# Tiles of 127 edges that carry the running sum in a row of their own, in a graph layer with two aggregations

## The reference

```python
def _L0_gnn_ref(x, edge_index, edge_attr, Wn, bn, We, be, attn):
    src, dst = (edge_index[0], edge_index[1])
    h = x @ Wn.T + bn
    e = edge_attr @ We.T + be
    ...
    a = jax.nn.leaky_relu(jnp.sum((xj + ee) * attn, axis=-1), NEG_SLOPE)
    m = jax.ops.segment_max(a, dst, num_segments=N)
    a = jnp.exp(a - m[dst])
    denom = jax.ops.segment_sum(a, dst, num_segments=N)
    a = a / (denom[dst] + 1e-16)
    msg = (xj * a[..., None]).reshape(-1, H * C)
    out = jax.ops.segment_sum(msg, dst, num_segments=N)
    return jax.nn.relu(out)

def _L1_gnn_ref(x, W1, b1, W2, b2, edge_index):
    dst = edge_index[0]
    nbr = edge_index[1]
    agg = jax.ops.segment_sum(x[nbr], dst, num_segments=n)
    cnt = jax.ops.segment_sum(jnp.ones((nbr.shape[0],), x.dtype), dst, num_segments=n)
    mean = agg / jnp.maximum(cnt, 1.0)[:, None]
    return x @ W1.T + b1 + mean @ W2.T + b2
edge_index = jnp.stack([src, dst])
x = _layernorm(x + _L0_gnn_ref(x, edge_index, edge_attr_128, ...), axis=-1)
x = _layernorm(x + _L1_gnn_ref(x, ..., edge_index), axis=-1)
```

## Time and profile before

| what | value |
|---|---|
| time, median of 3 runs | 1420.48 us (1420.19 to 1420.97) |
| the profiled execution: own time, span | 1415.41 us, 1413.6 us |
| TensorE busy (matmuls), its granted clock | 1191.4 us (84%), 0.945 |
| DVE, ScalarE, Pool busy | 1066.7, 737.7, 751.0 us |
| stage over destinations | about 394 to 618 us |
| dense stage | about 618 to 1034 us |
| stage over sources | about 1034 to 1386 us |

### The profile page before, as it was taken

How to read it: one execution, slowest core, us unless ns; L and a number is a source line. 1 busy time by engine, 2 the same in 40 slices (tenths; PEclk the granted TensorE clock), 3 DMA queues, 4 the chain that set the end, 5 groups by cost and what they waited for, 6 DMA issues and landing times.

```text
span 1413.6 us, 25643 instructions
## 1 busy us (share of the span) xinstructions
PE 1191.4 (84%) x6726; PEld 1029.3 (73%) x6726; DVE 1066.7 (75%) x3862; ACT 737.7 (52%) x1768; POOL 751.0 (53%) x731
## 2 busy tenths in 40 slices
PE   4499867980079999949999999999989998889894
PEld 3388756870068888838888888888878887778783
DVE  8988876887465555439999999999988877676761
ACT  4756684540034444427777777777764444343441
POOL 1057761777767777754444203556541656555663
PEclk9899998995589999979999999999999999999997
DMA  5988798979436666556777768999971332322221
GB/s 187 274 220 211 181 284 240 302 239 378 157 57 95 95 91 102 71 123 234 243 238 244 250 241 276 320 323 331 321 250 55 100 94 77 93 84 93 88 77 44
DMA packets 118435, 260.94 MB, mean 185 GB/s; under 512 B 23531, under 2 KB 57148, under 8 KB 118360
## 3 DMA queue, kind: packets, MB, share of 16 engines
q1 hardware_dynamic: 75738, 193.82, 43.1%
q0 software_dynamic: 40128, 64.45, 19.9%
q10 hardware_dynamic: 2494, 1.84, 0.4%
HBM read 182.48 MB, written 130.49 MB: 221 GB/s over the span
## 4 chain that ended last, share of the span: by engine, by line
PE 54%; DMA 11%; POOL 10%; issue 9%; DVE 7%; ACT 7%; ACTq 0%; POOLq 0%; DVEq 0%
PE bank L1261 31%; PE bank L1250 8%; DMA xin<-z_scratch,idx_src 5%; PE bank L1238 5%; POOL out_rows L469 4%; POOL xin L466 4%; PE bank L1313 4%; PE bank L1309 4%; ACT aggn L607 3%; DVE X L752 2%; DMA X<-in_x,idx_src 2%; PE bank L1189 2%; DVE stats L935 2%; DMA yout<-low_digits_scratch 2%; ACT sel L655 1%
## 5 line engine op out<-in xcount | busy, mean ns | idle before, releaser
L1261 PE MATMUL bank<-w1T,xT 128*128 128x256 f32 x1968 | 459.2, 380 | 0.3 <-ACT yout L569 0.3
L1261 PEld LDWEIGHTS bank<-w1T,xT 128*128 128x128 f32 x1968 | 366.1, 190 | 47.5 <-issue 0.9
L475 POOL DMA_INDIRECT order_scratch<-pay,rank_i x200 | 194.6, 973 | 221.7 <-DVE xin L752 89.9
L935 DVE BATCH_NORM_STATS2 stats<-xin 128x6 f32<-128x512 f32 x246 | 158.7, 687 | 88.6 <-DMA xin<-z_scratch,idx_src 67.0
L559 ACT ACTIVATE xT<-bank 128x512 f32<-128x512 f32 x346 | 207.3, 600 | 19.8 <-PE bank L1250 11.5
L569 ACT ACTIVATE yout<-bank,rstd 128x256 f32<-128x256 f32 x492 | 204.9, 484 | 5.7 <-DVE rstd L1151 5.2
L668 ACT COPY agg<-bank 128x257 f32<-128x257 f32 (+1 forms) x200 | 74.3, 371 | 220.5 <-PE bank L1313 214.4
L935 DVE BATCH_NORM_STATS2 stats<-bank 128x6 f32<-128x512 f32 x246 | 168.2, 693 | 23.7 <-PE bank L1261 23.7
L514 POOL DMA_INDIRECT z_scratch<-xin,idx_out x100 | 156.5, 1565 | 53.4 <-ACT xin L681 30.2
L564 ACT ACTIVATE std<-stats,eps_c 128x4 f32<-128x4 f32 x271 | 80.6, 298 | 179.3 <-DVE stats L935 177.0
L469 POOL DMA_INDIRECT out_rows<-yout,idx_out x100 | 99.8, 998 | 138.2 <-DMA xin<-z_scratch,idx_src 72.7
(11 more groups left out here) (199 smaller groups left out, 1766.5 us busy)
## 6 DMA issues: line engine op xcount, KB each, us to landing
z_scratch<-in_x SPq DMA_DIRECT2D x125, 400.0 KB
xin<-z_scratch SPq DMA_DIRECT2D x97, 512.0 KB
out_rows<-yout SPq DMA_DIRECT2D x97, 512.0 KB, 3.3
yout<-keys_scratch SPq DMA_DIRECT2D x50, 256.0 KB, 5.2
kB<-sorted_scratch SPq DMA_DIRECT2D x50, 256.0 KB, 3.4
yout<-low_digits_scratch SPq DMA_DIRECT2D x50, 128.0 KB
xin<-in_edge_attr SPq DMA_DIRECT2D x12, 512.0 KB, 5.3
order_scratch<-pay,rank_i POOLq DMA_INDIRECT x200
```

What stands on the lines that cost most here:

```text
L475: g.indirect_dma_start(out=order_dram[k], out_offset=bass.IndirectOffsetOnAxis(ap=rank_i[k][:, t:t + 1], axis=0), in_=pay[:, t, :], in_off ...
L935: return v.bn_stats(stats[0:rows, slot, 2 * p:2 * p + 2, :].rearrange("p j s -> p (j s)"), pair.rearrange("p j c -> p c j"))
L1261: ins = mm(to, buf[:, jj, c, 0:n], w[:, c, :], start=not biased and i == 0 and c == 0, stop=i == len(terms) - 1 and c == 1)
```

## The change

- **Tiles of 127 edges.** The ranks are raised by one (`offs` plus one), so record 0 of the sorted order is empty, and `load_order` reads windows of 128 records that start every `TW` = 127: row 0 of a tile repeats the last edge of the tile before. There are 100 tiles still. Row 0 of `X` is overwritten with the running sum, with weight one: ScalarE's `carry_row` copies row 0 of the bank (1 partition by 257) into row 0 of the next tile of `X`. For that the key row that goes to DRAM for the columns (`krowo`) has the tile's last key in column 0, so the column 0 of the product is the running sum of the last key.
- **One product per tile.** `csel`, `agg`, `prevk`, `lastrow` and the second product are gone; `select` makes four matrices per group instead of eight.
- **Scaling from PSUM.** In the first aggregation DVE's `dst_mean` takes a tile at a time from the bank (addition, reciprocal, scaling). In the second, DVE makes the reciprocal only (`src_count`) and ScalarE scales (`mean`). The next use of the bank waits for this (`s_an`) instead of for a copy. The column of means is gone (`XW` = 257).
- **Order.** TensorE's aggregations are spread between turns and half products, ScalarE's and DVE's instructions are put in another order, with the outputs in two halves.
- **Pool waits a group behind.** In the source stage the gathers of group `q` wait for the landing of those of `q - 1`, and the scatters of `h` for the landing of those of `h - 1`; the wait for the gathers just issued is gone.

```diff
-XW = D + 2
+XW = D + 1
+TW = P - 1
...
+                o = order_dram[k]
+                windows = bass.AP(o.tensor, o.offset, [[TW * 3, T], [3, P], [1, 3]])
+                pool.dma_start(ordrow[:], windows).then_inc(s_ord, 16)
+
+            pool.wait_ge(s_zero, 112)
             load_order(DST)
...
+                    if q >= 1:
+                        pool.wait_ge(s_xs[(q - 1) % 4], 16 * GT * ((q - 1) // 4 + 1))
                     for j in range(GT):
                         gather(xin[(G + q) % 4][:, j, :], z_dram, column(idx_src[SRC], GT * q + j), s_xs[q % 4])
...
                     pool.wait_ge(s_ey, GT * h + GT)
-                    if q < Q:
-                        pool.wait_ge(s_xs[q % 4], 16 * GT * (q // 4 + 1))
+                    if h >= 1:
+                        pool.wait_ge(s_ysc[(h - 1) % 4], 16 * GT * ((h - 1) // 4 + 1))
...
-            def raw(k, q, u, j):
-                act.wait_ge(s_agg[k], q * GT + j + 1)
-                wait(act, s_an[k], 2 * (q - 1))
-                w = D + 1 + k
-                a.copy(agg[u % 2][:, j, 0:w], bank[2 + j % 2][:, 0:w]).then_inc(s_raw[k], 1)
+            def carry_row(k, q, j):
+
+                t = q * GT + j
+                if isinstance(t, int) and t == T - 1:
+                    return
+                act.wait_ge(s_agg[k], t + 1)
+                if k == SRC and j == GT - 1:
+                    act.wait_ge(s_sel[SRC], q + 2)
+                a.copy(X[0:1, bass.ds(t + 1, 1), :].rearrange("p a c -> p (a c)"),
+                       bank[2 + j % 2][0:1, 0:XW]).then_inc(s_raw[k], 1)
...
+                def mean(j):
+                    if in_range(q, 0, Q):
+                        if j % 2 == 0:
+                            wait(act, s_tb[SRC], 2 * (q - 1) + j // 2 + 1)
+                        act.wait_ge(s_den[SRC], q * GT + j + 1)
+                        a.activation(aggn[:, j, :], bank[2 + j % 2][:, 0:D], ACT.Copy,
+                                     scale=den[:, 1, j:j + 1]).then_inc(s_an[SRC], 1)
...
+                row(0)
+                cp(0)
+                row(1)
+                cp(1)
                 if in_range(q, 2, Q + 2):
...
+                    root(2 + u % 2, s_est, q - 1, s_esq)
+                mean(0)
+                mean(1)
+                row(2)
+                if in_range(q, 0, Q):
+                    root(u % 2, s_ost, q + 1, s_osq)
+                y_pair(0)
+                mean(2)
+                row(3)
+                mean(3)
+                y_pair(1)
+                if in_range(q, 0, Q - 2):
+                    root_neighbours(q + 2, u)
...
+            def dst_mean(q, j):
+
+                o = bank[2 + j % 2]
+                t = q * GT + j
+                free_bank(DST, t)
+                ts(den[:, 0, j:j + 1], o[:, D:XW], TINY, None, ALU.add).then_inc(s_den[DST], 1)
+                dve.wait_ge(s_den[DST], 2 * t + 1)
+                v.reciprocal(den[:, 1, j:j + 1], den[:, 0, j:j + 1]).then_inc(s_den[DST], 1)
+                if j % 2 == 0:
+                    wait(dve, s_tb[DST], 2 * (q - 1) + j // 2 + 1)
+                dve.wait_ge(s_den[DST], 2 * t + 2)
+                ts(aggn[:, j, :], o[:, 0:D], den[:, 1, j:j + 1], None, ALU.mult).then_inc(s_an[DST], 1)
+
+            def src_count(q, j):
+
+                free_bank(SRC, q * GT + j)
+                wait(dve, s_an[SRC], GT * (q - 1) + j + 1)
+                v.reciprocal(den[:, 1, j:j + 1], bank[2 + j % 2][:, D:XW]).then_inc(s_den[SRC], 1)
...
+                wait(pe, s_an[k], t - 1)
+                wait(pe, s_raw[k], t)
+                rows = X[:, bass.ds(t, 1), :].rearrange("p a c -> p (a c)")
+                mm(bank[2 + j % 2][:, 0:XW], sel[u % 2][:, j, :], rows, start=True, stop=True).then_inc(s_agg[k], 1)
...
+                agg_(0)
+                turn_b(0)
+                turn_x(0)
+                agg_(1)
+                turn_b(1)
+                turn_x(1)
+                prod(0, 0)
+                agg_(2)
+                prod(0, 1)
+                agg_(3)
+                prod(1, 0)
+                prod(1, 1)
             steps(pe, Q + 2, 4, 4, 3, by_src)
```

232 lines of the change are left out of this document (109 added, 123 removed).

## The result

The changed kernel takes 1335.53 us (median of 4 runs, 1332.91 to 1337.76), the kernel before 1420.34 us beside it (1418.86 to 1420.97): a ratio of 0.9404, 95% interval 0.9385 to 0.9422. The forecast was 1343 us in a range of 1329 to 1375. The execution that was profiled took 1335.28 us for a span of 1333.5 us.

What follows compares the result with a forecast made beforehand. TensorE paces destinations, close ahead of Pool; in the source stage no engine is full and gather landings stall Pool and DVE. 1415.4 - 19 - 57.7 - 1.5 + 0.5 = 1337.7, plus 5.1 to the median: 1343 us, range 1329 to 1375.

Steps and rivals of the forecast that it cites:

- preparation: Before the first aggregation: more small DVE steps when the sorted rows arrive, +0.5 us, bounds 0 and +2.
- destinations: Stage over destinations: Pool's 100 adds in a row, 1.87 us apart, set the pace; -19 us, bounds -15 to -21.
- source run-in: Source groups 0 and 1: wait for ScalarE in both versions, fewer selections and products give perhaps 1.5 us: -1.5.
- source groups: Source stage: 10.8 us a group instead of 13.31, over 23 groups, -57.7 us; bounds 10.4 and 12.1 a group.
- run-out: End of the source stage (turn, products, statistics, outputs, last scatters): no edit shortens it, 0 us.
- the step on the start: Start of the destination stage: cold first tiles wait for ScalarE either way; first add at about 410.5 instead of 412.23 us.
- this mechanism as a rival: Destination stage: TensorE's standing lowers its clock to 1.2 GHz throughout, +138 us, 1481 us in all; chance 0.04.
- The walk through the group: One source group, engine by engine: TensorE's last product ends at 10.7 us; ScalarE and DVE keep about 1 us.
- both waits are met on arrival: Pool, source stage: gathers land in 2.7 to 4.2 us, with 5.2 us of other issues between, so its moved waits cost nothing.
- In-order stalls in the source stage: Rival, source stage: DVE's first statistics 1.3 us late make a group 12.1 us, 1373 us in all; chance 0.18.
- Pool's instructions lengthen: Rival, source stage: all eight Pool instructions at the longest need 11.7 us a group, 1364 us in all; chance 0.07.
- The landing stays on the path: Rival, source stage: gathers reach DVE late, loop stays near 13.3 us, only destinations gain, 1400 us; chance 0.07.

Runs made afterwards that it cites:

- experiment 4: Changed kernel with two of Pool's four scatter-adds per destination group left out, so half the rows are not added: 1313.05 us, ratio 0.9241.
- experiments 8 and 9: Changed kernel plus unread bf16 products of zeros before and between TensorE's first aggregations, run twice: 1331.28 and 1331.22 us, against 1335.22 us for the changed kernel.
- experiment 3: Changed kernel with TensorE making every aggregation product twice into the same bank: 1399.42 us, ratio 0.9845.
- experiment 6: Changed kernel with ScalarE copying the running sum's row twice, first to a spare row: 1353.38 us, ratio 0.9517.
- experiment 1: Changed kernel with Pool's old wait back: source-stage scatters again wait for the gathers just issued. 1380.52 us, ratio 0.9716.
- experiment 2: Kernel before with only Pool's new source-stage waits, a group behind; old tiles and two products a tile kept: 1394.9 us, ratio 0.9812.

## Why the prediction was right, and by how much

The prediction took 77.7 us off the profiled execution; it is 80.1 in the spans, and 80.1 in the times (1415.4 to 1335.3). The forecast of 1343 us lies 7.5 us above the median of 1335.5 all the same: 4.8 of that is the step from the profiled execution to the median, 5.1 us in the kernel before (1415.4 to 1420.5) and 0.3 in the changed one (1335.28 to 1335.53). That the sum itself is off by 2.4 us only is in part luck, as the destination stage fell 4.5 us short and the source stage gave 6.7 more:

| term | forecast | measured | how |
|---|---|---|---|
| preparation | +0.5 | +0.4 | first aggregation 397.38 against 396.99 |
| destinations | -19 | -14.5 | dense loads -14.1, less the preparation |
| source run-in | -1.5 | -3.8 | end of group 1's products 17.9 us earlier, less the 14.1 |
| source groups | -57.7 | -62.1 | 23 x (13.31 - 10.61), the latter from 1060.17 to 1304.22 us |
| run-out | 0 | 0 | 29.3 us against 29.4 from the last group's turns to the end |

**Destinations, the mis-sized term.** The steps on the pace were right: adds 1.87 us apart with nothing between, TensorE's group of 6.7 us (experiment 4). What failed is the step on the start, "the first tiles, with TensorE still cold, wait for ScalarE in either version", with the first add at 410.5 us. It came at 415.45, and the term is 14.5 us, just outside its bounds of 15 to 21. From the first aggregation to the first add the change made it 2.8 us longer (18.1 against 15.2), where I had it some 1.7 shorter. Before, a product that needed no copy ran while ScalarE copied, TensorE had no gap, and the granted clock rose at some 400 us. After, the one product waits for the copy; TensorE stood 0.55 us behind each of the first ones, and the clock rose at some 410 us. The 1.16 us that the prediction gives the chain from tile to tile were read at 401.53 us, with the clock already up: it was 1.74 us at the lower level and 1.21 with the products of zeros. Products of zeros in the gaps take 5.0 us of it back (experiments 8 and 9), about as much as the 4.9 us by which the first add came late. The Trainium skill (TensorE: Matmul & The Clock Gate, section "What's actually happening") has the lower clock as the default and activity as what lifts it. These runs agree so far: 0.50 from 380 to 397 us in both kernels, where TensorE had little to do, and 1.00 from 392 to 412 us with the products of zeros. But it isn't the amount of work alone: in experiment 3 TensorE makes two products a tile, with the same stands, and the clock came no sooner.

I had this mechanism as a rival, in the wrong place: that the standing of 1 us in 7.5 would let the clock fall all through the stage, at +138 us. That case never arose, as TensorE doesn't stand group by group but runs ahead and stands at the end: the granted clock is 1.00 in every window from 412 to 580 us, 0.55 from 580 to 590 and 0.50 after, with no work left. So the price of 138 us was not put to the test. At the start of the dense stage the clock is at its lower level in both kernels (0.50 from 604 to 612 us after, 0.50 from 618 to 626 us before), so that costs nothing new. The clock that was lost is that of the start, before it had risen at all.

**Run-in.** Of the 3.8 us, 1.4 are there already at the first source aggregation (1038.56 against 1054.04 us, 15.5 earlier), the rest by the end of group 1's products (1060.17 against 1078.04 us). The sign was right, and more came than the 1.5 us forecast. What is left there is in part the clock, at 0.53 from 1041 to 1052 us, of which experiments 8 and 9 take back 2.2 us.

**Source groups.** The walk through the group gave 10.7 us, I took 10.8, and it is 10.6; so both stalls that I had allowed for were smaller. One group of the changed kernel, all engines:

```profile
1155.61 0.60 PE L1357 MATMUL bank<-X,sel 128*128 x2
...
1156.68 1.09 ACT L560 ACTIVATE xT<-bank 128x512 f32<-128x512 f32 x2
1156.92 0.61 PE L1357 MATMUL bank<-X,sel 128*128 x2
...
1157.37 0.62 PE L1300 MATMUL bank<-ident,aggn 128*128 128x128 f32 x4
...
1159.26 0.83 ACT L746 ACTIVATE aggn<-bank,den 128x256 f32<-128x256 f32 x2
...
1160.11 0.65 PE L1357 MATMUL bank<-X,sel 128*128 x2
```

From the first aggregation: the second at 1.31 us (walk: 1.3), the means of tiles 0 and 1 at 3.65 to 4.48 us (walk: 4.2 to 5.0), the third aggregation at 4.50 us (walk: 4.6). It starts straight behind TensorE's half product and not because a mean has come: ScalarE was some 0.5 us ahead of the walk, as two instructions of one form behind each other took 1.09 us for two turned copies of 0.60. TensorE loses 0.2 us a group, at the weight load of the turns ("PEld bank L1300 <- ACT xT L560", 3.8 us in 17 times), where the walk had 0.3. The slack of about 1 us that the walk gives ScalarE fits experiment 6, which finds some 1.5 in the chain.

**The move of Pool's wait** did what the prediction says ("both waits are met on arrival"), and the landing stayed off the path; experiment 1 prices it at 42.0 us in the 24 steps and experiment 2 at 26.8 with the old tiles.

**The signs named beforehand.** Adds 1.87 us apart, no wait of DVE for a gather and Pool's unbroken row came as written; the dense loads came at 604.14 us and not near 599, and the source groups at 10.6 us, just under the 10.7 to 10.9. One sign of being wrong was met: a granted clock below 0.95 after 400 us (0.50 from 400 to 408 us, 0.71 from 408 to 412). It points at the step on the start.

**The rivals.** In-order stalls in the source stage: TensorE is busy 180 of 180 us. Pool's instructions lengthen: gathers had a median of 965 ns (942 to 1047, 1070 to 1300 us) where it was 976 (942 to 1167), scatters a median of 1005 ns in both. Eight of them with 0.30 us each between make 10.3 us (the prediction has 10.4 from the same rows) in a group of 10.6, so there are 0.3 us in hand, and no more. The rule on the shared port (the Trainium skill, SBUF — State Buffer, section "SBUF: two separate sides") would have let both grow shorter; one did and one did not, so these runs neither show it nor exclude it. The landing stays on the path: that is experiment 1's kernel, not this one.

**Small steps.** The one-row copy costs 361 ns and the copy of 128 rows cost 366, so the upper bound that I took holds. DVE's scaling in the destination stage takes 484 ns from PSUM and took 444 from SBUF (means of 420 to 590 us), where I had no surcharge; 0.16 us a group, hidden, as DVE is busy 12.5 of 20 us (480 to 500 us). The Trainium skill (VectorE: DVE Perf Modes, section "The TRN2 errata — SBUF-src ops pay a fixed extra latency per instruction") gives VectorE a fixed term of 58 cycles from SBUF and 120 from PSUM; at its 0.96 GHz the difference is 65 ns, as an estimate. The measured 40 ns is less, and decides.

## What to carry to other kernels

When one edit relieves an engine and another relieves a wait, neither may show much alone: build the table of both, each, and neither (here 26.8, 21.1 and 63.1 us). Look at the pace group by group before taking a mean, since the first groups can run at another bound. And when a product is taken out that TensorE made while another engine worked on the link of the chain, look at the granted clock at the start of the stage: with a stand in its place what remains ran at half speed for some 12 us here, and products of zeros that nobody reads bought 4.0 us of the time back.

## What was not expected of the hardware

TensorE's clock at the start went with the stands of the chain: with 1.20 us of product in each 1.74 for five tiles, and hardly a gap after, it stayed at 1.2 GHz from 397.4 to some 409.8 us. With two products a tile and the same stands (experiment 3) it stayed there from 400.8 to some 417 us, while with no stand at all it rose between 397.0 and 400.5 us (before). The end of the preparation, before the first aggregation, moved between 397.1 and 400.8 us from run to run of kernels that don't differ there. And at the end of the stage over sources the new wait of Pool for the scatters of the group before shows a little:

```profile
1310.30 0.98 POOL L466 DMA_INDIRECT out_rows<-yout,idx_out  x1 [2.23 <-DMA out_rows<-yout,idx_out]
```

In the last groups there are no gathers in between to cover the landing. It isn't on the path in the changed kernel, where the last group's scatters wait for ScalarE (1317.89 us).
